# A cross-attention block on one core: transposes before a pair's first scores, and four chunks of fc2 behind the last pair's hT

## What is computed

```python
def layer_norm(x, w, b):
    mu = jnp.mean(x, axis=-1, keepdims=True)
    var = jnp.var(x, axis=-1, keepdims=True)
    return (x - mu) * jax.lax.rsqrt(var + EPS) * w + b
B, N, C = x.shape                      # 32, 256, 256
M = context.shape[1]                   # 77
H = 16
D = C // H
xq = layer_norm(x, qn_w, qn_b)
ctx = layer_norm(context, cn_w, cn_b)
q = (xq @ q_w).reshape(B, N, H, D)
kv = (ctx @ kv_w).reshape(B, M, 2, H, D)
k, v = (kv[:, :, 0], kv[:, :, 1])
attn = jnp.einsum('bnhd,bmhd->bhnm', q, k) * scale
attn = jnp.where(xa_mask[:, None, :, :], neg, attn)
attn = jax.nn.softmax(attn, axis=-1)
out = jnp.einsum('bhnm,bmhd->bnhd', attn, v).reshape(B, N, C)
x = x + (out @ proj_w + proj_b)
h = layer_norm(x, n2_w, n2_b)
h = jax.nn.gelu(h @ fc1_w + fc1_b, approximate=False) @ fc2_w + fc2_b
return x + h
```

## Time and profile before

| | us |
|---|---|
| median of 3 runs | 822.07 |
| lowest, highest | 819.4, 825.85 |
| the profiled execution | 826.84 |
| its span, first to last instruction | 825.0 |

### The profile page before, as it was taken

One profiled execution on the slowest core, in us unless ns is written; L12 is line 12 of the kernel. 1 busy time (PEld: TensorE's weight loads), 2 busy tenths in 40 slices (PEclk: granted clock), 3 DMA queues, 4 the chain that ended last, 5 costly groups with the idle time before them and its releaser, 6 DMA issues.

```text
span 825.0 us, 16989 instructions
## 1 busy us (share of the span) xinstructions
PE 772.6 (94%) x5615; PEld 635.2 (77%) x5615; DVE 606.2 (73%) x1379; ACT 560.0 (68%) x781; POOL 180.1 (22%) x185
## 2 busy tenths in 40 slices
PE   6748899999999999999999999999999999999998
PEld 6635769788786978778796978879697887869587
DVE  5737768788787869877786877778686877868453
ACT  4607776777777677777677777667767777776832
POOL 2311122221202222220222222021222212021230
PEclk9759999999999999999999999999999999999999
DMA  7767649395775939385684939477493947639100
GB/s 234 150 93 159 76 146 147 104 137 116 142 119 139 126 117 144 96 158 102 149 115 136 136 94 159 92 162 102 150 139 105 141 104 151 111 101 133 31 27 25
DMA packets 89478, 100.47 MB, mean 122 GB/s; under 512 B 9060, under 2 KB 63576, under 8 KB 89432
## 3 DMA queue, kind: packets, MB, share of 16 engines
q1 hardware_dynamic: 88694, 99.55, 63.1%
q10 hardware_dynamic: 754, 0.53, 0.4%
HBM read 69.22 MB, written 30.83 MB: 121 GB/s over the span
## 4 chain that ended last, share of the span: by engine, by line
PE 65%; DMA 13%; issue 10%; ACT 5%; DVE 4%; POOL 2%; ACTq 1%; SPq 0%; DVEq 0%; POOLq 0%
PE A L863 13%; DMA QM<-sd 8%; PE F L863 8%; PE ST L933 8%; PE A L942 7%; PE F L987 7%; PE F L989 6%; PE F L988 6%; DMA sd<-cT_lo 3%; PE ST L915 3%; ACT g_hi L542 2%; PE A L958 2%; DMA xin<-in_x 1%; PE A L877 1%; PE A L915 1%
## 5 line engine op out<-in xcount | busy, mean ns | idle before, releaser
L508 ACT ACTIVATE probs<-ST 78x512 f32<-78x512 f32 x256 | 137.3, 588 | 67.0 <-PE ST L933 66.6
L987 PE MATMUL F<-w_hi,g_hi 128*128 128x256 f32 x480 | 142.9, 298 | 0.0
L988 PE MATMUL F<-w_lo,g_hi 128*128 128x256 f32 x480 | 134.0, 279 | 0.0
L989 PE MATMUL F<-w_hi,g_lo 128*128 128x256 f32 x480 | 133.9, 279 | 0.0
L594 DVE TENSOR_TENSOR g_lo<-g_f,g_hi 128x512 fp32r<-128x512 f32 x128 | 95.7, 748 | 33.5 <-ACT g_hi L542 30.7
L528 ACT ACTIVATE QM<-mask_u 77x2048 fp32r<-77x2048 uint8 x64 | 116.8, 1896 | 0.0
L933 PE MATMUL ST<-QM,KM 127*78 127x256 f32 x512 | 90.4, 293 | 19.0 <-DMA QM<-sd 18.2
L423 POOL TENSOR_TENSOR xin<-xin,projb 128x1024 f32<-128x1024 f32 x16 | 38.3, 2393 | 318.1 <-DMA xin<-in_x 318.1
L987 PEld LDWEIGHTS F<-w_hi,g_hi 128*128 128x128 f32 x480 | 90.4, 188 | 18.5 <-issue 18.5
L933 PEld LDWEIGHTS ST<-QM,KM 127*78 127x78 f32 x512 | 61.3, 148 | 56.1 <-ACT probs L508 26.7
L434 POOL TENSOR_TENSOR oT_lo<-g_f,oT_hi 128x512 fp32r<-128x512 f32 x32 | 41.2, 1287 | 245.0 <-ACT oT_hi L515 245.0
(11 more groups left out here) (168 smaller groups left out, 1842.1 us busy)
## 6 DMA issues: line engine op xcount, KB each, us to landing
QM<-qd SPq DMA_DIRECT2D x48, 512.0 KB, 14.4
xa<-in_x SPq DMA_DIRECT2D x16, 512.0 KB, 3.9
qd<-q_hi SPq DMA_DIRECT2D x32, 256.0 KB, 2.2
qd<-q_lo SPq DMA_DIRECT2D x32, 256.0 KB, 2.1
xin<-in_x SPq DMA_DIRECT2D x16, 512.0 KB, 5.1
QR<-qd SPq DMA_DIRECT2D x16, 480.0 KB, 5.2
out<-xin SPq DMA_DIRECT2D x30, 256.0 KB, 6.4
KM<-kd SPq DMA_DIRECT2D x48, 156.0 KB, 6.9
```

Of the source, the lines that this page charges most:

```text
L508: act.activation(probs[:, quad % NSLOT, 2 * (p % 2):2 * (p % 2) + 2], ST[p % 2][0:MX].rearrange("p (h n) -> p h n", n=N), ACT.Exp, scale=S ...
L987: pe.matmul(dst, g_hi[:, k, tok], w2_hi[:, k], start=(k == 0), stop=False)
L988: pe.matmul(dst, g_hi[:, k, tok], w2_lo[:, k], start=False, stop=False)
L989: last = pe.matmul(dst, g_lo[:, k, tok], w2_hi[:, k], start=False, stop=(k == HC - 1))
```

## The change

In pairs 0 to 14 the transposes of ctx and x for the next pair stand ahead of the first scores, and part 1 of x comes before part 0, on TensorE and in VectorE's splits (also in the set-up). In the last pair three of the six early chunks of fc2 stand ahead of the first scores. In the last pair the chunks 4 to 7 of fc2's last token tile stand behind the transposes `hT`. There `fc1(15, 0)` waits only for the first half of VectorE's additions, `fc1(15, 1)` for the second, and VectorE adds the second half behind `hT_low`.

```diff
@@ -633,9 +633,10 @@
                 low(cT_lo[:], cT_cols, cT_hi[:]).then_inc(cT_lo_done, 1)
 
             def xT_split(j, k):
-                dve.wait_ge(xT_mm, KC * j + k + 1)
+                n = KC * j + KC - k
+                dve.wait_ge(xT_mm, n)
                 dve.tensor_copy(xT_hi[:, k], XT[k][:]).then_inc(xT_hi_done, 1)
-                dve.wait_ge(xT_hi_done, KC * j + k + 1)
+                dve.wait_ge(xT_hi_done, n)
                 low(xT_lo[:, k], XT[k][:], xT_hi[:, k]).then_inc(xT_lo_done, 1)
 
             def k_low(j):
@@ -762,10 +763,10 @@
             dve.wait_ge(bias_mm, 1)
             dve.tensor_copy(bias[:, 0:2 * G], ST[1][:, 0:2 * G]).then_inc(setup_done, 1)
             cT_split(0)
-            xT_split(0, 0)
+            xT_split(0, 1)
             for k in range(KC):
                 weight_low(qw_lo[:, k], raw_q[:, k], qw_hi[:, k], 0, k, KC + k + 1)
-            xT_split(0, 1)
+            xT_split(0, 0)
             for k in range(KC):
                 dve.tensor_scalar(bv_in[:, k], count[:, 0], vecs[:, 3, k:k + 1], None, ALU.mult).then_inc(bv_in_done, 1)
             k_low(0)
@@ -791,8 +792,8 @@
             def body(j, par, mlp, prep, ahead):
                 if prep:
                     cT_split(j + 1)
+                    xT_split(j + 1, 1)
                     xT_split(j + 1, 0)
-                    xT_split(j + 1, 1)
                 if mlp:
                     g_low(j - 1, HC - 1)
                 if prep:
@@ -825,10 +826,12 @@
                 if prep:
                     for r in range(4, 8):
                         row_max(j + 1, r)
-                if mlp:
+                if mlp and prep:
                     add_x1(j - 1, 1 - par, 1)
                 hT_low(j, 0)
                 hT_low(j, 1)
+                if not prep:
+                    add_x1(j - 1, 1 - par, 1)
                 if prep:
                     for r in range(8, RBANKS):
                         row_max(j + 1, r)
@@ -1019,8 +1022,8 @@
             bias_columns(ST[1], raw_q, 1, 0, G)
             bias_columns(ST[1], raw_kv, 3, G, G).then_inc(bias_mm, 1)
             cT(0)
+            xT(0, 1)
             xT(0, 0)
-            xT(0, 1)
             pe.wait_ge(cT_lo_done, 1)
             pe.wait_ge(setup_done, 2 + 1)
             k_proj(0)
@@ -1046,18 +1049,22 @@
             def body(j, par, mlp, prep, ahead):
 
                 pe.wait_ge(hT_lo_done, KC * j)
+                pe.wait_ge(v_done, j + 1)
+                if prep:
+                    cT(j + 1)
+                    pe.wait_ge(shiftT_done, j + 1)
+                    xT(j + 1, 1)
+                    pe.wait_ge(gelu_done, least(HC * j - 1))
+                    xT(j + 1, 0)
+                early = 3 if prep else HC - 2
+                ahead_of_scores = 0 if prep else 3
+                if mlp:
+                    for k in range(ahead_of_scores):
+                        fc2(j - 1, 0, k)
                 scores(j, 0)
                 scores(j, 1)
-                pe.wait_ge(v_done, j + 1)
-                if prep:
-                    cT(j + 1)
-                    pe.wait_ge(gelu_done, least(HC * j - 1))
-                    xT(j + 1, 0)
-                    pe.wait_ge(shiftT_done, j + 1)
-                    xT(j + 1, 1)
-                early = 3 if prep else HC - 2
                 if mlp:
-                    for k in range(early):
+                    for k in range(ahead_of_scores, early):
                         fc2(j - 1, 0, k)
                 scores(j, 2)
                 scores(j, 3)
@@ -1121,7 +1128,7 @@
                 project(j, 1)
                 for t in (2, 3):
                     for k in range(HC):
-                        if mlp and 4 * t + k // 2 > 8:
+                        if mlp and 4 * t + k // 2 > 8 and (prep or t < 3 or k < HC - 4):
                             fc2(j - 1, t, k)
                         if not mlp and k % 2:
                             keep_warm(F[0], 1)
@@ -1137,9 +1144,14 @@
                     maxima(j + 1, 9)
                 pe.wait_ge(setup_done, ALL_READY)
                 pe.wait_ge(setup2_done, 4)
-                pe.wait_ge(y_done, 2 * j)
+                if not prep:
+                    for k in range(HC - 4, HC):
+                        fc2(j - 1, 3, k)
+                pe.wait_ge(y_done, 2 * j if prep else 2 * j - 1)
                 pe.wait_ge(hT_lo_done, KC * (j + 1))
                 fc1(j, 0)
+                if not prep:
+                    pe.wait_ge(y_done, 2 * j)
                 if prep:
                     maxima(j + 1, 10)
                     maxima(j + 1, 11)
```

More of the change, by code:

```diff
@@ L1048, in body @@
                 pe.wait_ge(hT_lo_done, KC * j)
-                scores(j, 0)
-                scores(j, 1)
                 pe.wait_ge(v_done, j + 1)
@@ L1053, in body @@
                     cT(j + 1)
+                    pe.wait_ge(shiftT_done, j + 1)
+                    xT(j + 1, 1)
                     pe.wait_ge(gelu_done, least(HC * j - 1))
                     xT(j + 1, 0)
-                    pe.wait_ge(shiftT_done, j + 1)
-                    xT(j + 1, 1)
                 early = 3 if prep else HC - 2
+                ahead_of_scores = 0 if prep else 3
                 if mlp:
-                    for k in range(early):
+                    for k in range(ahead_of_scores):
+                        fc2(j - 1, 0, k)
+                scores(j, 0)
+                scores(j, 1)
+                if mlp:
+                    for k in range(ahead_of_scores, early):
                         fc2(j - 1, 0, k)
```

## The result

The changed kernel took 812.64 us (median of 4 runs, 810.04 to 813.17), and the kernel before took 821.22 us beside it (median of 4, 819.4 to 825.85): a ratio of 0.9877 with a 95% interval of 0.9845 to 0.991. That is 8.6 us faster, against the forecast of 809.0 us (804.5 to 814.5). The profiled execution of the changed kernel is the lowest of its four, 810.04 us with a span of 808.2; the one shown of before, 826.84 us with a span of 825.0, is above all four of its runs. So the spans differ by 16.8 us, the medians by half of that, and a part of what follows is about this difference.

A forecast was written before the change was run, and what follows sets the result against it. TensorE was taken to be bound by waiting before each pair's first scores for the transfer into QM. Gains of 11.9 + 0.3 + 1.0 + 0.95 = 14.2 us led to 809.0 us, range 804.5 to 814.5.

The forecast's parts named there:

- The gap was worth its length, less what the exps hold: Pairs 1 to 14, wait before first scores: moving transposes there gains the gap less 0.27 us each, 11.9 us in all.
- the sum: Whole kernel: 11.9 + 0.3 + 1.0 + 0.95 = 14.2 us off the profiled execution's 825.0 span; chance 0.70.
- The new wait: TensorE before scores 3, each pair: a new wait for exps, some 0.3 to 0.5 us a pair.
- The cap: Pairs 1 to 14: the gain never exceeds 1.07 us, reached for gaps over 1.34.
- Kept further on: Behind the K projection: operands are ready in time (Q projection with 0.57 us of cover), so the gain is kept.
- The last pair: Last pair: 1.0 us from three fc2 chunks ahead of the scores, 0.95 us from four chunks behind the hT transposes.
- The first pair: First pair, transposes ahead of scores at a lower TensorE clock: gain between 0 and 0.6, taken as 0.3 us.
- From the sum to the median: Profiled execution to median: the 4.8 us above the median was taken to lie mostly outside the gaps, giving 809.0.
- rival (a): Gaps before the first scores: they are shorter in undisturbed runs, so the time is 812.3 us; chance 0.18.
- (b): Later half of the scores: if ScalarE sets the pace there, half the pairs' gain goes back, 815 us; chance 0.06.
- (c): Pair starts: earlier ctx and x loads delay the QM transfer; landing 1.5 us later gives 826 us; chance 0.04.
- (d): Pair starts: TensorE's clock falls to half as transposes and waits stand together, 840 us or more; chance 0.02.

The follow-up runs named there:

- e6: The changed kernel with four small extra exps on ScalarE between the table load and each pair's first exp: 815.77 us, ratio 0.9912 to the kernel before.
- e5: The kernel before with four small extra exps on ScalarE between the table load and each pair's first exp: 824.1 us, ratio 1.0007 to the kernel before.
- e4: The changed kernel run once more, unchanged: 812.32 us, ratio 0.9851 to the kernel before.
- e12: The changed kernel with one tiny 512 B transfer issued on SP ahead of the loads of QM: 819.93 us, ratio 0.9949 to the kernel before.
- e1: The kernel before run once more, unchanged, for a second trace: 826.02 us, ratio 1.0004.
- e3: The kernel before with only the last pair's parts of the change: 824.51 us, ratio 0.9991 to the kernel before.
- e2: The kernel before with only the transposes moved in pairs 0 to 14, last pair left as it was: 815.06 us, ratio 0.9864.
- e9: The changed kernel with one chunk of fc2 put between scores 2 and 3, later chunks moved up: 810.82 us, ratio 0.9926 to the kernel before.
- e10: The changed kernel with the first pair's first scores again ahead of the transposes: 813.37 us, ratio 0.995 to the kernel before.
- e11: The kernel before with one tiny 512 B transfer issued on SP ahead of the loads of QM: 842.41 us, ratio 1.0222 to the kernel before.

## Why the prediction held, point by point

**The gap was worth its length, less what the exps hold.** Right. The forecast put the K projection at F + 3.49 and it is at F + 3.56; it moved by 0.81 in the mean and each pair became 0.81 shorter (11.34 over 14), where 0.85 was forecast. The second exp ends at F + 3.21 as forecast; of the missing 0.07, 0.01 is the hand-over from it to scores 3 (0.05 for 0.04) and 0.06 the way from there to the K projection (0.30 for 0.24). One reading was wrong without harm to the sum: ScalarE's last gelu doesn't end at F, it starts there and takes 0.69 us; the sum used F + 2.15 as a whole. That the first exp's time, F + 2.15, would not move was right in all 14 pairs, and e6 against e5 shows that it is now what holds. The row shows why it is that early: the exp starts 1.41 us after the table load does (569.56 to 570.97), as before (580.67 to 582.08). The Trainium skill (ScalarE: Activation LUTs, What ACT_TABLE_LOAD costs) has about 2.66 us for a switch, by which nothing would have been gained; the trace disagrees, and the measured gain with it.

**The new wait.** It is there, in the rows of the weight loads: 0.57 us in pairs with early landings as pair 9, nothing in pair 11, and 0.41 a pair in the mean, for the 0.3 to 0.5 forecast (0.23 in e4, whose landings are later). It comes in two halves, and not at scores 3 alone. The step took TensorE to scores 2 at F + 2.67, when the first exp is nearly done; with an early landing it comes some 0.2 earlier and waits there too. The list of waits by matmuls has 0.7 us of it in all.

**The cap.** The forecast was F + g + 2.15 from a gap of 1.34 on; e12 gives 2.05 to 2.08 behind it, from about 1.5 on. The time of the moved transposes was taken as 1.07 and the distance shrinks by 1.14. It cost nothing here, since nearly all landings are earlier.

**Kept further on.** Right: K projection 0.81 earlier, pair 0.81 shorter. The Q projection starts at F + 6.00 in every pair, 2.44 after the K projection, as before the change, so it didn't find xT_lo late. But that behind it "everything hangs on TensorE" does not hold in every pair. The load of QR comes in too: in the traces of the kernel before it lands 1.2 to 1.35 us ahead of the first maxima that read it (means of before, e1, e3, e5), in those of the changed kernel and of e2, e9 and e10 0.2 to 0.85. It takes the same 5.6 to 5.8 us from issue to landing; its lead has shrunk, because its issue did not come earlier by as much as the maxima did. Where the lead is gone TensorE waits, and part of the gain goes back: nothing in the changed kernel's first trace, 0.6 us in e4, 1.0 in e2, 1.8 in e9 and 3.4 in e10, and in none of the 14 pairs of before, e1, e3, e5 and e11. The sum put this at nothing.

**The last pair.** 2.29 for 1.95 forecast. The four chunks end just before fc1, whose wait is 0.25, as forecast to be within 0.5. The start brought 1.36 where 1.0 was forecast: the next exp starts at F + 3.28 and not F + 4.64. But its landing was also 0.37 earlier than in the profiled execution of before. In e3, with a landing like that of before (F + 1.62 for F + 1.57), this exp starts at F + 3.66, which is 1.0 earlier, and the whole is 2.0.

**The first pair.** 0.3 forecast; not measured, as e10 tells.

**From the sum to the median.** This was the weak step. Sum and trace agree (11.34 + 2.29 = 13.6 for the 11.9 + 1.95 forecast, the start's scatter left out), but the median fell by 8.6 in the first comparison, by 12.5 in the second and by 3.8 in e10's. The text leant to the view that what the profiled execution had above the median lay elsewhere than in the gaps, which gave 809.0. The changed kernel came out at 812.64 and 812.32, the number of rival (a), 812.3, while the one before had medians of 821.2 to 824.8, and 817.2 on one chip. That the number fits doesn't show the reason of (a), short gaps in undisturbed runs: the 4.8 us above the median were in one execution, and of the part that traces can compare (e3 and before) more lies in the start than in the gaps. On the other side the changed kernel's own profiled execution, 2.6 below its median, had the earliest start of its six traces (102.64, mean 103.8) and no wait for QR. So that the time fell within the range is the mechanism's merit; how near it came to 809.0 in any one comparison is in part luck. Of the 817.2 no cause is shown: no trace of before was taken on that chip, and in e10's own trace there the landings are at F + 1.26 in the mean, not early.

**The other rivals.** (b) as told is out: the exps of the later half give nothing back; what goes back goes by way of QR, as said. (c) is out. The load of ctx is issued at F + 0.45 to 0.47 and that of x at F + 1.37 (read in two pairs), so in most pairs the first meets the end of QM's transfer. Yet this transfer took 4.5 us from issue to landing in the mean and 4.8 in e4, for 4.8 and 4.9 in the two traces of before. e12 shows its mechanism at the forecast price, one to one behind the slack. (d) did not come: in the changed kernel, and in e12 with stands of up to 1.19 us behind the transposes, the K projection comes at the same distance in every pair, which a fall of the clock would stretch. e11 shows such falls in the kernel before, with stands 0.65 us longer in the mean.

## What to carry to other kernels

Work that needs nothing of a transfer belongs ahead of the wait for it; its worth is the gap less what the next chain (here a table load and two exps, counted from where the engine before it ends) will hold, and that chain can be read in the trace beforehand. Beside the saved time the pairs become deaf to the transfer's scatter up to a slack that can be worked out. Look also for the next transfer that TensorE will meet once it comes earlier (here QR, with a lead of 1.2 us that fell to 0.2 in the worst trace). And compare with a median and a spread of before, not with one profiled execution. Once the next chain holds, filling its wait brings far less than the wait's length (e9: 0.1 us in early pairs, nothing over all).

## What the runs showed of the hardware

- A stand of TensorE can cost more than its length. After stands of 1.84, 2.15, 2.35 and 2.40 us in e11 the granted clock fell to its lower level for some 3 us and that cost 1.3 to 1.56 us more; after six others of 1.84 to 2.22 us it stayed. What tells them apart is open.
- The load of QM takes 3.5 to 5.2 us from issue to landing for the same bytes at the same place in the pair. In the kernel before that scatter goes into the length of each pair.
- The load of the maxima operand QR became late in single pairs once the pairs were shorter. e4 has one such pair, which lasts 47.23 instead of 46.63; TensorE's row there:

```profile
219.82 0.71 PE L918 MATMUL ST<-KR,QR 125*128 125x234 f32 x4 [0.62 <-DMA QR<-qd]
```

  In e10 the list has the most of it:

```profile
PE ST L918 <- DMA QR<-qd: 5.4, 6, 2.2
```

  The longest, 2.2 us, is in the start of the program, where every trace has one of 1.0 us or more; those within later pairs are what the changed kernel still has of scatter there.
- A transfer of 512 B takes SP 0.62 us of issue, so even tiny transfers ahead of a late one are paid for.
